# Gate logits out of the aggregation's and the values' products, instead of from transposed rows

## The reference, cut to what matters

```python
t = tokens(x)                                  # 8 x 1024 x 256
z = _ln_t(t)                                   # layer norm of each row
qkv = z @ w_qkv.T                              # q, k, v, 8 heads of 32
sa = softmax(q k / sqrt(32)) v
t = t + sa @ w_agg.T + b_agg
z2 = _ln_t(t)                                  # the rows behind the attention
gate_logits = z2 @ gate_weight                 # 256 x 8
gates = sinkhorn(log(clip(gate_logits, 1e-6))) # 8 iterations over tokens and experts
vals, idx = top_k(gates.T, 128)                # each expert picks 128 tokens of a batch
t[idx] += (z2[idx] @ experts[e]) * vals
```

## Time and profile before

| | |
|---|---|
| median of 3 runs (lowest to highest) | 1469.12 us (1467.42 to 1470.44) |
| profiled execution, its span | 1467.7 us, 1.4 us under the median; no time of its own beside the span is given for it |
| TensorE busy | 1339.3 us, 91% |
| VectorE busy | 1021.3 us, 70% |
| ScalarE busy | 868.7 us, 59% |
| GpSimd busy | 562.6 us, 38% |
| mean granted clock of TensorE | 0.950 |

### The profile page before, as it was taken

How to read it: one execution, slowest core, us unless ns; L and a number is a source line. 1 busy time by engine, 2 the same in 40 slices (tenths; PEclk the granted TensorE clock), 3 DMA queues, 4 the chain that set the end, 5 groups by cost and what they waited for, 6 DMA issues and landing times.

```text
span 1467.7 us, 29142 instructions
## 1 busy us (share of the span) xinstructions
PE 1339.3 (91%) x10849; PEld 915.8 (62%) x10849; DVE 1021.3 (70%) x2114; ACT 868.7 (59%) x1268; POOL 562.6 (38%) x1068
## 2 busy tenths in 40 slices
PE   5789989999999999999999999999998999987535
PEld 3556656667576767676767676656666567766423
DVE  3536766858585857586768676787789776899771
ACT  2456557677667767677666767665675667542100
POOL 1132530445134513551245214520554116875443
PEclk9899989999999999999999999999999999999665
DMA  2051013600360037002710272005500265454322
GB/s 79 29 137 51 1 30 87 172 16 27 80 184 15 2 93 193 18 2 75 184 46 2 57 168 79 2 30 117 144 15 2 65 169 191 128 158 134 118 68 80
DMA packets 66785, 119.13 MB, mean 81 GB/s; under 512 B 10705, under 2 KB 46546, under 8 KB 66642
## 3 DMA queue, kind: packets, MB, share of 16 engines
q1 hardware_dynamic: 57682, 90.48, 22.9%
q0 software_dynamic: 8960, 26.75, 6.0%
HBM read 29.11 MB, written 33.55 MB: 43 GB/s over the span
## 4 chain that ended last, share of the span: by engine, by line
PE 62%; DVE 24%; issue 6%; POOL 4%; ACT 3%; DMA 0%; DVEq 0%; POOLq 0%; ACTq 0%
PE shared L938 30%; PE scores L894 12%; PE acc L916 11%; DVE prob_sum L1635 6%; PE acc L913 3%; PE shared L933 3%; DVE acc_sb L1609 2%; DVE bn L1344 2%; ACT probs L1209 2%; DVE work L1543 1%; PE acc L926 1%; DVE resid L1350 1%; DVE best_i L1541 1%; DVE best L1539 1%; DVE bn_x L1404 1%
## 5 line engine op out<-in xcount | busy, mean ns | idle before, releaser
L1209 ACT ACTIVATE probs<-scores 128x1024 f32<-128x1024 f32 x512 | 516.0, 1024 | 178.1 <-PE scores L894 94.0
L894 PE MATMUL scores<-query_stack,key_stack 96*128 96x256 f32 x2048 | 342.1, 308 | 16.0 <-ACT probs L1209 15.7
L1635 DVE TENSOR_TENSOR prob_sum<-prob_sum,probs 128x512 f32<-128x512 f32 x512 | 331.3, 707 | 0.0
L894 PEld LDWEIGHTS scores<-query_stack,key_stack 96*128 96x128 f32 x2048 | 275.9, 192 | 85.1 <-issue 39.1
L916 PE MATMUL acc<-probs,v_all 128*32 128x256 f32 x4096 | 289.2, 389 | 0.0
L1242 POOL TENSOR_TENSOR attn_T<-acc_sb 128x256 f32<-128x256 f32 x56 | 41.4, 740 | 447.8 <-DVE acc_sb L1609 445.0
L938 PE MATMUL shared<-w_sb,chan 128*128 128x512 f32 (+1 forms) x512 | 186.7, 501 | 5.9 <-DVE chan L1438 5.9
L916 PEld LDWEIGHTS acc<-probs,v_all 128*32 128x32 f32 x4096 | 114.8, 110 | 104.0 <-issue 37.9
L938 PEld LDWEIGHTS shared<-w_sb,chan 128*128 128x128 f32 x512 | 91.9, 192 | 62.5 <-issue 57.9
L938 PE MATMUL shared<-chan,w1T 128*128 128x512 f32 x256 | 121.3, 608 | 2.1 <-ACT chan L1125 2.1
L1635 DVE TENSOR_TENSOR prob_sum<-probs 128x512 f32<-128x512 f32 x128 | 98.4, 810 | 18.8 <-ACT probs L1209 16.5
(11 more groups left out here) (220 smaller groups left out, 2036.7 us busy)
## 6 DMA issues: line engine op xcount, KB each, us to landing
query_stack<-hi SPq DMA_DIRECT2D x120, 128.0 KB, 2.5
key_stack<-hi SPq DMA_DIRECT2D x120, 128.0 KB, 2.5
x_sb<-in_x_dram SPq DMA_DIRECT2D x8, 1024.0 KB, 5.3
out_dram<-resid SPq DMA_DIRECT2D x16, 512.0 KB, 4.8
tokens_scratch<-resid SPq DMA_DIRECT2D x16, 512.0 KB, 5.5
tokens_scratch<-rows SPq DMA_DIRECT2D x16, 512.0 KB, 3.3
key_stack<-lo SPq DMA_DIRECT2D x60, 128.0 KB, 2.5
query_stack<-lo SPq DMA_DIRECT2D x60, 128.0 KB, 2.5
```

Source lines behind the costliest of these rows:

```text
L894: last = pe.matmul(score_ps[u % 2][:, QB * r:QB * (r + 1)], key_stack[stack, HG * g + r, P * kt:P * (kt + 1)], query_stack[stack, HG * g + ...
L1209: act.activation(probs[:, u % PROBS, :], score_ps[u % 2][:, :], ACT.Exp, scale=DH ** -0.5) \
L1635: dve.tensor_tensor(total[:, part], probs[:, (u - 1) % PROBS, part] if kt == 1 else total[:, part], probs[:, u % PROBS, part], ALU.add).th ...
```

## The change

The layer norm is linear but for the row's mean m and its factor r: z2 @ W = r * (t @ W - m * sum(W)). And t is the sum of the aggregation's product, the bias, and the linear attention's output, whose own product with W can be had beside the values. So 8 columns are added to two products:

- The aggregation's stationary data stay, and its moving weights `waggT` get 8 more columns, `w_agg.T @ W` (64 products a batch of 264 columns in place of 256, with the values').
- The weights of the values `w1T` get the 8 columns W. Here the rows are normalized with the front's mean and factor, so ScalarE copies the 8 columns with the row's deviation as scale (`ln_s`), and VectorE adds mean and bias terms (`deviations`, `means`).
- VectorE adds the two parts in `agg` (one addition of 8 columns for a tile), and the step `logits` corrects by mean and factor and clips, for four tiles at a time: four linked instructions. It waits for the row factor, not for the rows.
- `z2T` and `gate` go: for a batch 16 transposes, 8 copies on ScalarE, 32 TensorE instructions of 8 columns, 8 clips.
- The step `v` is now one tile (8 steps of weight 0.9 in place of 4 of 1.8), with two ScalarE instructions for a tile.
- Two steps in the first front make the extra weights (`gate_weights`, `gate_sums`), and 3 more small loads bring data for them.
- The list of steps is written anew around this: a rest of 2 becomes 1.5, one of 1 becomes 0.5, and the sum of the weights falls from 94.6 to 88.4, so steps lie closer in slots.

```diff
-             ("gvar",), ("store_stats", 1), ("z2T", 0), ("store_rows", 3), ("z2T", 1), ("z2T", 2), ("z2T", 3),
-             ("xn", 0), ("gate", 0), ("rest", 2), ("qk0", 0), ("gate", 1), ("store_rows", 4), ("qk0", 1), ("xn", 1),
-             ("gate", 2), ("store_rows", 5), ("z2T", 4), ("rest", 1), ("store_rows", 6), ("qk0", 2), ("gate", 3),
...
+             ("gvar",), ("store_stats", 1), ("store_rows", 3), ("logits", 0), ("xn", 0), ("rest", 1.5),
+             ("qk0", 0), ("store_rows", 4), ("qk0", 1), ("xn", 1),
+             ("store_rows", 5), ("rest", 0.5), ("store_rows", 6), ("qk0", 2),
...
-    segments[1].chains = [(0.5, 16, squares, segments[0])]
+    segments[1].chains = [(0.5, 12, squares, segments[0])]
...
-                    last = product(ps[:, 0:C], [(attn_T[:, c, tok[at[0]]], waggT[:, c, :]) for c in range(CH)])
-                elif kind == "z2T":
-                    pe.wait_ge(s["z2_ready"], T * seg.stores + at[0] + 1)
-                    last = transposes(ps, *(rows[:, at[0], half[c]] for c in range(CH)))
-                elif kind == "gate":
-                    await_read(pe, seg, "z2T", at[0])
-                    await_small(pe)
-                    last = product(ps[:, 0:E], [(z2T[:, c, tok[at[0]]], gate_w[:, c, :]) for c in range(CH)])
+                    last = product(ps[:, 0:C + E], [(attn_T[:, c, tok[at[0]]], waggT[:, c, :]) for c in range(CH)])
...
-                    for j in range(2):
-                        last = product(ps[:, C * j:C * (j + 1)],
-                                       [(chan[:, c, tok[2 * at[0] + j]], w1T[:, c, 2 * C:3 * C]) for c in range(CH)])
+                    last = product(ps[:, 0:C + E], [(chan[:, c, tok[at[0]]], w1T[:, c, 2 * C:3 * C + E])
+                                                    for c in range(CH)])
...
+                    act.activation(v_all[:, 0:G + 1:G, t, :], ps[:, 0:C].rearrange("p (g n) -> p g n", g=G), ACT.Copy)
+                    logits = gates[:, 0 if shifted_by_max else seg.front, t, :]
+                    read(act.activation(logits, ps[:, C:C + E], ACT.Copy, scale=ln_s[:, t:t + 1]), seg, *st)
...
+                if kind == "agg":
+                    logits = logits_of(seg.store)[:, t, :]
+                    last = dve.tensor_tensor(logits, ps[:, C:C + E], logits, ALU.add)
...
+                elif kind == "logits":
+
+                    dve.wait_ge(s["row_r_ready"], stored + at[0] + 1)
+                    part = slice(T // 2 * at[0], T // 2 * (at[0] + 1))
+                    logits, means = logits_of(seg.store)[:, part, :], mean_part[:, part, :]
+                    link(means_times_sums(means, part))
+                    link(dve.tensor_tensor(logits, logits, means, ALU.subtract))
+                    link(dve.tensor_tensor(logits, logits, ln_r[:, part].unsqueeze(2).to_broadcast([P, T // 2, E]),
+                                           ALU.mult))
+                    dve.tensor_scalar(logits, logits, CLIP, None, ALU.max).then_inc(s["logits_ready"], 1)
...
+                elif kind == "deviations":
+                    dve.wait_ge(s["row_r_ready"], stored + 2 * seg.has("store") + 2)
+                    dve.tensor_tensor(ln_s[:, :], ln_v[:, :], ln_r[:, :], ALU.mult).then_inc(s["deviations_ready"], 1)
```

More of the change, by code:

```diff
@@ L86, in order @@
 def order(attend, front, store):
-    store_part = {"agg", "store_stats", "store_rows", "z2T", "gate"}
+    store_part = {"agg", "store_stats", "store_rows", "logits"}
     attend_part = {"resid"}
@@ L118, in first_order @@
 def first_order():
-    steps = [x for x in order(False, True, False) if x[0] not in ("zT", "proj", "v", "square", "norms")]
+    steps = [x for x in order(False, True, False) if x[0] not in ("zT", "proj", "v", "deviations", "means", "square", "norms")]
     rows = [steps.index(("front_rows", t)) for t in range(T)]
@@ L359, in build_attention @@
     qT = hi[:, 0:2, :]
-    z2T = hi[:, 2:4, :]
     qk0 = lo[:, :, :].rearrange("p j n -> p (j n)").rearrange("p (t n) -> p t n", n=2 * C)
@@ L1009, in step @@
                     last = product(ps[:, 0:C], [(ones[0:1, :], env["bagg_row"])])
+                elif kind == "gate_weights":
+                    await_small(pe)
+                    pe.wait_ge(s["to_turn_in"], 48)
+                    for c in range(CH):
+                        last = product(ps[:, E * c:E * (c + 1)],
+                                       [(env["wagg_nat"][:, o, half[c]], gate_w[:, o, 0:E]) for o in range(CH)])
+                elif kind == "gate_sums":
+                    pe.wait_ge(s["gate_bias_ready"], 1)
+                    last = product(ps[:, 0:2 * E], [(ones[:, :], gate_w[:, c, :]) for c in range(CH)])
                 elif kind == "proj":
@@ L1034, in step @@
                     elif store_of:
-                        for t in range(T - 2, T):
-                            await_read(pe, store_of[routing.groups[g][1] - 1], "gate", t)
+                        pe.wait_ge(s["logits_ready"], 2 * (store_of[routing.groups[g][1] - 1].stores + 1))
                     else:
@@ L1384, in row_deviations, with logits_of, means_times_sums @@
                                          op1=ALU.mult).then_inc(s["row_r_ready"], 1)
+            def logits_of(b):
+                return gates[:, 0 if shifted_by_max else b, :, :]
+            def means_times_sums(out, part):
+                tiles = part.stop - part.start
+                return dve.tensor_tensor(out, mv[:, part, 0].unsqueeze(2).to_broadcast([P, tiles, E]),
+                                         gate_sums[:, 0:E].unsqueeze(1).to_broadcast([P, tiles, E]), ALU.mult)
             def step(seg, st):
```

113 lines of the change are left out of this document (68 added, 45 removed), and 6 rows, old and new, of the table steps.

## The result

The changed kernel takes 1542.58 us (median of 4 runs, 1542.13 to 1543.73) against 1468.76 (4 runs, 1467.42 to 1470.44): ratio 1.051, interval 1.0488 to 1.0533. It is slower, as predicted, but by 74 us instead of 41, and so outside the range of 1458 to 1533. The profiled span is 1541.1 us at a granted clock of 0.926 (before 1467.7 at 0.950).

The account below looks back on a forecast made before the run. TensorE was taken as the bound, without slack in six attentions. A batch: -4.8 + 4.0 + 2.0 + 3.5 + 2.0 = +6.7; six make +40.2, the rest +1, giving 1510 us, 2.8% slower; range 1458 to 1533.

Parts of the forecast that it names:

- What bounds the kernel: Six of eight attentions: TensorE runs end to end, so work removed and new waits both count in full.
- The removed work, -4.8 us: TensorE: gate products and transposes gone, less the added columns, saves 4.8 us a batch in seven attentions.
- First wait: From gvar to the first qk0: TensorE waits 4.0 us for xn behind GpSimd's chain; bounds 1.5 to 4.5.
- Second wait: Same place, slot 7: score product waits 2.0 us more for an exponential behind the fifth row tile; bounds 0 to 2.3.
- Second place: From lin (slot 21) to zT: TensorE waits 3.5 us for VectorE's additions, an exponential and row tile; bounds 1.5 to 4.
- The clock: Half-clock stretches behind the waits at both places: 2.0 us a batch, 0.3 at the first, 1.7 at the second; bounds 0 to 6.
- First attention: Attention without a store: the second place and a shorter first one, +4 us (0 to 7).
- First front: Start of the kernel: two steps with handovers and four more ScalarE instructions, +2 us (0 to 3).
- The last attention: Saves the 4.8 but steps stand behind later routing ones and row factors behind GpSimd's gathers: -2 us (-4.8 to +3).
- Behind it: After the last attention: rows, transposes, copies and gates leave the way to the routing, -3 us (-6 to 0).
- More waits than I found: Rival: agg's extra addition holds PSUM banks, means holds VectorE, low clock counts in full: 1533 to 1560, chance 0.09.
- The faster rival: TensorE's work decides: waits at the two places absent or under 4.8 us a batch; 1434 to 1453, chance 0.15.

Follow-up runs that it names:

- squeezed_before: The kernel before, its work unchanged, with its other steps dealt into the slots they have in the changed kernel: 1578.83 us, ratio 1.0759 to before.
- rows_later: spaced with row tiles 4 to 6 one slot later on ScalarE, behind the copies of the second and third qk0: 1452.4 us, ratio 0.9897 to before.
- rows_later_gmean: rows_later with agg 7 moved from ahead of gmean to behind it: 1449.88 us, ratio 0.988 to before.
- spaced: The changed kernel with empty steps of the old weights where transposes and gate products stood, and the earlier rests: 1483.67 us, ratio 1.0107 to before.
- second_place: The changed kernel with one slot more between front_rows_3 and zT, taken from the rest at the segment's end: 1523.45 us.
- gate_setup_later: rows_later_gmean with the first front's gate_weights and gate_sums moved behind the first two transposes to chan: 1446.8 us, ratio 0.9868 to before.
- first_place: The changed kernel with one slot more between xn and the first qk0, taken from the rests behind head_scale_1: 1531.13 us.
- lin_later: The changed kernel with one slot more ahead of the first qk0 (as in first_place) and one ahead of lin 4, from the end rest: 1518.88 us.
- all_later: The changed kernel with all steps from the first qk0 on one slot later, taken from the segment's end rest: 1493.05 us, ratio 1.021 to before.
- no_corrections: spaced without VectorE's eight additions of gate columns in agg and the one of means, so logits lack these terms: 1476.11 us.

## Why the prediction was right and wrong

**What bounds the kernel: right.** TensorE has no slack in the six segments, and the waits came on. It shows in squeezed_before and, the other way round, in rows_later.

**The removed work, -4.8 us: right.** rows_later_gmean has a period 4.1 under that of before, and its waits make 1.0 us where those of before made 0.6: 4.5 without them. With the isolated figure of the Trainium skill, in "TensorE: Matmul & The Clock Gate", section "Back-to-back issue gap", it would have been 2.1; the section itself says that this figure counts too little in a stream with weight loads. The runs decide for the 0.11 us an instruction of the earlier trace rows.

**First wait, +4.0: right.** `xn` came when said: `qk0` at T+6.3, forecast T+6.2, so next to 2.2 us of work the place costs 4.1. The row shows only 2.9 of it: TensorE was there at T+3.4 (620.27 less 2.91), not T+2.2, because the score product ahead of it waited 0.6 us for its exponential and the halts made the rows between 0.6 us longer than I had summed.

**Second wait, +2.0: wrong here, right in its mechanism.** The row tile ran at T+13.4 and its exponential ended at T+15.5, as said, but TensorE came to it at T+15.4 and not at T+13.4: `qk0` at half the clock had taken 1.7 us more, and some 0.1 of the 2.0 was left. It showed in full once the first wait was mended (spaced, 3.2 us), and rows_later took it away: 31 us with the half clock behind it. A wait on a path can hide the next one, which is paid when the first is cured.

**Second place, +3.5: right.** Slot 21 starts at 693.15 (X) and `zT` at 703.65, X+10.5 as forecast, against 7.0 us of work. Of the 3.5, 2.4 are the wait for `rows`, 0.4 one for an exponential (700.52), and the rest is spread over the groups between; in second_place the wait for `rows` was gone.

**The clock, +2.0: 3.4, and not where I had it.** Two stretches of 3.4 us, both full of work on the path, 1.7 each. The Trainium skill ("TensorE: Matmul & The Clock Gate", section "HAM oscillation — how this bites in real kernels") charges half of the throttled time, and by that rule, the trace agrees: 3.43 us for four products that take 1.72. I had hidden most of the first stretch behind the second wait; it took that wait's place instead. The 1.7 that I had put behind the second place did not come: the clock stayed at 1.00 behind its 2.39 us. A stretch of the same size came behind the third place, which I didn't have, so that a part of this term is right by luck.

**The step that failed: two places were taken for all.** In "What bounds the kernel now" I went through the timeline "at the places where TensorE was only just supplied" and stopped at two. The change takes 6.4 of the weights that share out 32 slots and 1.0 of the rests, so every step up to slot 31 moved by up to one, about 4.7 us, and at least three more places were near their limit: the second half of `zT` (2.1 us and a stretch of low clock), the transposes of `lo` (0.8) and the block's total (0.7). Rebuilt from the rows of after, the sum a segment is -4.8 + 4.1 + 0.1 + 3.5 + 2.1 + 1.5 + 3.4 = 9.9 against 10.4 measured; the last 0.5 is in delays of under 0.5 us that I have not divided. Of this the unnamed places make 5.3 (2.1 + 1.5 and 1.7 of the clock), while 1.9 of the second wait and the low clock at the second place, both in the forecast, did not come. By the table above the forecast is 31 us short: 23 in these six segments (63.0 to 40.2), 3 each in the first front, the first attention and the last.

**Outside the segments.** First attention +7.0, at the upper bound of 0 to 7. First front +5.0, outside 0 to 3: the twelve products and two copies of the gate's setup stand ahead of VectorE's head scaling (half of it or more, by gate_setup_later). The last attention +1.2, within -4.8 to +3. Behind it -3.7, forecast -3: near, though TensorE waits 10 us for `logits_1` there; the first sum came 2.2 us sooner behind the last aggregation product, where I had said some 3. That this is because the transposes and gate products are gone from that stretch is argued.

**The rivals.** That VectorE's additions cost nothing as load was right (105.2 us busy in 160), as delay they cost 0.5 a segment; "More waits than I found" was the case that came, at a chance of 0.09, and its range of 1533 to 1560 held for other reasons than those it gave: `means` had no part in it that a run shows, the additions had 0.5 a segment, and the stretches of half clock cost 3.4 and not 6. The faster rival was the right answer for another order of the same work: gate_setup_later, at 1446.8, lies in the 1434 to 1453 that I had given it.

## What to carry to other kernels

Where weights deal steps over slots, taking a step out moves all the others: leave its slot empty first, measure, and only then close up. When TensorE is bound end to end, look at every step whose input comes just in time, not at the two nearest to the edit; a row for the wait ahead of each step, in order of its size, is the list. And a wait of 2 to 3 us can bring half clock behind it, which here cost another 1.7 behind two of three such waits.

## What the runs showed of the hardware

The granted clock fell behind some waits and not behind others, and the length of the wait alone does not tell them apart.

- In the steady segments of the changed kernel it fell to 0.50 for 3.4 us behind 2.91 us of waiting (busy 0.36 of 3 us) and behind 2.14 (0.28 of 2), every time, and stayed at 1.00 behind 2.39, every time. In first_place the same wait, 2.38 us at 693.94, had such a stretch behind it.
- In lin_later four short waits (0.63, 0.60, 0.89 and 0.67 us, from 448 to 457 us) stood ahead of such a stretch; they come again in each of five segments, and the stretch followed in three of them (at 457, 774 and 931 us) and not in two (about 302 and 615 us). In all_later the same four come in five segments, and the clock is 1.00 from 280 to 990 us, with waits of up to 1.8 us in it.
- Single waits for the keys in lin_later: 1.80 us, up to 579.93, had no such stretch behind it, 2.09, up to 736.59, had.
- The wait of 3.1 us for an exponential in no_corrections had a stretch behind it four times and none the first time (296.09 us, clock 1.00 from 295 to 301).

In the prediction I gave the waits of 2 us and more their share of low clock; that several short ones can bring it too, and that one of 3.1 can stay without it, I had not expected. What decides was not tried.
